# Experts' products in pairs, their rows turned by way of HBM, and the next attention's projections begun between them

## The chip, the cores and the metric

One NeuronCore of a Trainium2 chip runs the whole kernel. The metric is the device time in microseconds (us) of one execution, as the median of several. Engines: TensorE (PE) multiplies, with its weight loads shown apart as PEld; VectorE (DVE), ScalarE (ACT) and GpSimd (POOL) work on elements; SyncE (SP) issues all transfers (DMA) here, in order.

## The reference, cut to what matters

The input is `x` of 8 x 64 rows of 512 and a context of 8 x 1601 rows. Two layers of (attention over the context, attention or a time-mixing block over `x`, a feed-forward block) follow one another. The change lies where layer 0 ends and layer 1 begins:

```python
# layer 0, feed-forward: groups of 16 rows; 64 experts (16 x 4), each picks one row of each group
logits = einsum('...btd,des->...btes', grouped, controller) + tie
perm   = (logits == max(logits, axis=-3, keepdims=True))
sel    = einsum('...btd,...btes->...besd', grouped, perm)
inner  = relu(einsum('...besd,desf->...besf', sel, f1) + bias)     # 512 -> 64 for each expert
inter  = einsum('...besf,esfd->...besd', inner, f2)                # 64 -> 512 for each expert
x      = x + einsum('...besd,...btes->...btd', inter, perm)
# layer 1, attention over the context: 16 heads of 32
q = norm(x) @ Wq.T;  k = ctx @ Wk.T;  v = ctx @ Wv.T
x = x + softmax(scale * q k^T) v @ Wp.T + bp
```

There are 512 rows, so 32 groups and 64 x 32 pairs of an expert with its row.

## The kernel before, in words

Each engine has its own program, and they meet at semaphores. Tiles are 128 partitions by up to 512 columns, and `X`, the running rows, is four tiles of 128 rows. `R` is one large area of SBUF that every stage lays out anew by word offsets. PSUM is two halves of four banks, `SC` and `SB` (its banks are `BK`).

The middle stages take the banks of `SB` in a fixed ring of four. `JOBS` lists them in order with the engine that reads each ("d" DVE, "a" ACT); `open_bank` waits until the bank's last reader is through, `filled` and `readout` are the two semaphore levels of a job, and `evacuate` copies the jobs of one name out on the engine named. So `inter` 0, 2, ... are read by DVE and 1, 3, ... by ACT. `running(pe, us)` puts dummy 128 x 128 products on PE.

The order of PE's program around the change:

1. `sel` (L1071): the chosen rows, transposed, into 16 banks.
2. `inner` (L1084): four banks `q`, eight pairs of experts `j` in each. A pair is computed in two halves `r` of 64 weight columns, one in each half of the array, in four passes `k` over the 512 inputs. DVE adds the bias and applies the relu, into `inner`, cleared before so that the other expert's half of the columns is zero.
3. `inter` (L1097): f2 is the weight operand, in halves of 64 columns, the pair's `inner` is streamed (64 columns). The result has the 512 outputs on partitions, so it is not yet by rows; 16 banks, copied into `intert`.
4. `intert` (L1103): 64 transposes of 128 x 128 in 16 banks, copied into `intern`, where the partition is (group parity, expert).
5. `combination` (L1108): four products for each tile of rows, with `permx`, the choice, as weights of 32 columns. Then for each tile DVE adds to `X` and makes the norm's statistics, ACT the root, DVE the scaled row (`norm`), PE transposes it (`norm_transposes`, L415), ACT makes its high part (`norm_out`) and DVE its low part (`norm_low`). `normed` runs this tile by tile, with dummy products while PE waits.
6. `q4` (L1123): the queries in three passes. Products of the attention are f32 split in a high and a low part, so that each is three faster products (`three_passes`, L431).
7. `FIRST4`: the keys and values of batch 0. The context arrives transposed in four pieces (`load_chunk`), ACT makes the high part ("h" steps), DVE the low one (`split_low`), and then come jobs ("k", (piece, output blocks)) read by ACT into `keys` and ("v", tile) read by DVE into `vals`, 12 instructions each at the full width, in a ring of three banks. The same list of steps is walked by each engine, each doing its part; letters in `CONTROL4` take no bank.
8. Seven batches `BATCH4` of attention with the next batch's projections between, then `LAST4`, which also holds the last layers.

SP's queue goes: f1 in four transfers, f2 after `y2` 3, the raw weights of keys and values (`wraw`) once `inner` 3 is filled, the queries' weights and the bias row once `inter` 15 is filled, and the chunks once `intert` 15 is filled. POOL makes the low parts of these weights (L734) and both parts of the queries' weights (`split_weight`).

Of the kernel before, what the change touches and what calls it, by code (L numbers as in the profile page):

```python
# [25 lines left out]
EP = E // 2  # L26
G = B * T // NE
# [138 lines left out]
FIRST4 = [("h", 0), ("q", 0)] + EARLY4 + [("g", 0)]  # L166
BATCH4 = [attention(LATE4 + EARLY4, begins=b == 0, ahead=b < B - 2) for b in range(B - 1)]
CONTROL4 = "sohgq-mbpzelRNrEUA0C"
# [80 lines left out]
def mid_jobs():  # L249
# [32 lines left out]
    add("intert", 16, "da")  # L282
# [11 lines left out]
def build(nc, x, ctx_, ctx_end, W0, vecs, Wk, Wv, Wr, Wo, ctrl, f1, f2, Wq4, Wk4, Wv4,  # L294
# [7 lines left out]
    with ExitStack() as es:  # L302
# [40 lines left out]
        tiecol = sb("tiecol", [E, 1])  # L343
# [5 lines left out]
        minus_round = sb("minus_round", [P, 1])  # L349

        SC = psum("SC", [P, 2048])
        SB = psum("SB", [P, 2048])
        BK = [SB[:, k * 512:(k + 1) * 512] for k in range(4)]

# [97 lines left out]
        def spread_choice(eng, tt, name):  # L452

            inc(eng.tensor_tensor(permb[:, tt, :, :], permn[:, tt, :].unsqueeze(2).to_broadcast([P, E, 8]),
                                  gmask[:, :].unsqueeze(1).to_broadcast([P, E, 8]), ALU.mult), name)

# [13 lines left out]
        def by_batch(v):  # L470
# [15 lines left out]
        inner = Z[:, 1, :].rearrange("p (a k) -> p a k", k=2 * G)  # L486
        sel = R3.rearrange("p a c n -> p (a c n)").rearrange("p (c e g) -> p c e g", c=NC, g=G)
        intert = view(24576, 8192, NC, G, E)
        intern = view(16384, 8192, G // 2, D)

# [5 lines left out]
        batch4 = KW + VALS  # L496
        keys = [view(u * batch4, KW, HP, HK) for u in range(2)]
        vals = [view(u * batch4 + KW, VALS, KT_N, D) for u in range(2)]
        free4 = 2 * batch4

        low = [R[:, free4 + k * 2048:free4 + (k + 1) * 2048] for k in range(2)]
        wraw = R3[:, 0], R3[:, 2]

        low_r = [float32r(f"low{k}", free4 + k * 2048) for k in range(2)]
        high_r = [float32r("high0", free4 + 4096), float32r("high1", LT_AT)]
        wlow = [float32r(f"wlow{w}", R3_AT + 2 * w * 2048).rearrange("p (c n) -> p c n", n=D) for w in range(2)]
        whigh = [float32r(f"whigh{w}", R3_AT + (2 * w + 1) * 2048).rearrange("p (c n) -> p c n", n=D) for w in range(2)]
        wq4 = view(14336, 2048, NC, D)
        wp4 = view(0, 2048, NC, D)

        wq4_low, wq4_high, norm3_low = (cols(float32r(*a)) for a in (("wq4_low", 14336), ("wq4_high", 0),
                                                                    ("norm3_low", 2048)))
        norm_high = cols(high_r[1])
# [21 lines left out]
        short_keys = view(free4 + 6144, HP * MR, HP, MR)  # L535

        short_words = view(free4 + 6144, HP * MR + T)
        sums_inv = view(free4 + 6144 + HP * MR + T, NC * T)
# [13 lines left out]
        dt = [view(a, 2048, NC, D) for a in (2048, 4096, 6144, 8192)]  # L552
        normed4 = view(10752, 3 * D, 3, D)
        on5 = view(12288, 512, 2, 256)
        v5 = R[:, free4:free4 + 4096].rearrange("p (b j n) -> p b j n", j=HP // 2, n=P)
        k5 = view(free4 + 4096, 2048, NC, B * T)
# [10 lines left out]
        wq8 = view(10240, 512).bitcast(mybir.dt.int8).rearrange("p (c n) -> p c n", n=D)  # L567
        wq32 = view(10240, 512).bitcast(mybir.dt.int32).rearrange("p (c n) -> p c n", n=D // 4)
        wqt = view(12800, 1024).bitcast(BF16).rearrange("p (c n) -> p c n", n=D)
        xqt = view(13824, 1024).bitcast(BF16).rearrange("p (c n) -> p c n", n=D)  # L570
        xq = view(14848, 2048, NT, D)
        y6 = view(16896, 2048, NT, D)
        wsrow = view(18944, 512)
        bqrow = view(19456, 512)
# [10 lines left out]
        def _(sp):  # L585
# [42 lines left out]
            inc(sp.dma_start(tiecol[:, :], tie), "cw_in", 16)  # L628
# [8 lines left out]
            sp.wait_ge(*filled("inner", 3))  # L637
            inc(sp.dma_start(wraw[0], natural(Wk4)), "wk4_in", 16)
            inc(sp.dma_start(wraw[1], natural(Wv4)), "wv4_in", 16)
            sp.wait_ge(*filled("inter", 15))  # L640
            inc(sp.dma_start(wq4, natural(Wq4)), "wq4_in", 16)
            inc(sp.dma_start(bprow, bp4.unsqueeze(0).to_broadcast([P, D])), "bp_in", 16)

            def load_chunk(b, c):
                n, at = NC * piece_n(c, 1), NC * piece_keys(c).start
                inc(sp.dma_start(low[c % 2][:, 0:n], ctxt[b, :, at:at + n]), f"chunk_in{c % 2}", 16)

# [10 lines left out]
            def load_batch(b):  # L658
                for c in range(KC):
# [7 lines left out]
            sp.wait_ge(*filled("intert", 15))  # L667
# [21 lines left out]
        def _(pool):  # L689
# [18 lines left out]
            def split_weight(pool, w, high, low, name):  # L708

                inc(pool.tensor_copy(high, w), name)  # L710
                pool.wait_ge(sem(name), 1)
                inc(pool.tensor_tensor(low, w, high.bitcast(F32), ALU.subtract), name)
# [19 lines left out]
            for w in range(2):  # L732
                pool.wait_ge(sem("whigh"), w + 1)
                inc(pool.tensor_tensor(wlow[w], wraw[w], whigh[w].bitcast(F32), ALU.subtract), "wlow")  # L734
# [191 lines left out]
        def inter_dst(n):  # L926
            q, c = n // 4, n % 4
            return (intert[:, c, :, 16 * q:16 * q + 16],
                    bank("inter", n)[:, :].rearrange("p (e g) -> p g e", g=G))

# [14 lines left out]
        def steps4(eng, run):  # L945

            run(FIRST4, None, None)
            for b in range(B - 1):
# [4 lines left out]
        def _(pe):  # L953
# [135 lines left out]
            running(pe, 1.6)  # L1089
            pe.wait_ge(sem("f2_in"), 16)  # L1090
            for q in range(4):
                pe.wait_ge(*readout("inner", q))
                for c in range(NC):
                    bk = open_bank(pe, "inter", 4 * q + c)
                    for j in range(8):
                        for r in range(2):
                            last = pe.matmul(bk[64 * r:64 * r + 64, j * 64:(j + 1) * 64],  # L1097
                                             f2s[:, 8 * q + j, c * P + 64 * r:c * P + 64 * r + 64],
                                             inner[:, 8 * q + j, :], start=True, stop=True)
                    last.then_inc(filled("inter", 4 * q + c)[0], 1)  # L1100
            running(pe, 0.6)
            all_read(pe, "inter", 16)
            for gp in range(G // 2):  # L1103
                transposes(pe, "intert", gp, [(intert[:, c, 2 * gp:2 * gp + 2, :].rearrange("p g e -> p (g e)"), P, P)
                                              for c in range(NC)])
            pe.wait_ge(sem("permx"), 2)

            def combination(tt):  # L1108
                for i in range(4):
# [722 lines left out]
```

## Time and profile before

| | |
|---|---|
| median of 3 runs | 1179.06 us (1177.03 to 1179.46) |
| the profiled execution | 1176.5 us, its span 1174.7 us |
| PE busy | 1133.5 us, 96% |
| DVE, ACT, POOL busy | 619.1, 432.8, 333.6 us |
| granted PE clock, mean | 0.994 |
| instructions | 35,100, of them 16,122 products |
| read from HBM, written | 112.44 MB, 1.05 MB |

The time is that of the execution, the span is from the first to the last instruction of the trace. PE's products are pipelined and a product's shown end is modelled, so the spacing of starts tells more than the durations: a product's time includes its way through the array, some 165 ns over its streaming. An f32 product is two instructions, which together pass its columns four times; a product of split parts (fp32r) is one instruction and passes them once.

### The profile page before, as it was taken

To read this page: it belongs to the slowest core of one execution; us is meant where nothing else is said; L and a number is where in the kernel's file an instruction comes from. 1 tells how busy PE (TensorE), PEld (TensorE's weight loads), DVE (VectorE), ACT (ScalarE), POOL (GpSimd) and SP (SyncE) were. 2 spreads that over 40 slices of the span, in tenths; PEclk is the share of its full clock that TensorE was granted. 3 is DMA by queue.
4 is the path that set the end of the run, shared out by engine and by line. 5 is a ranking of instruction groups with operands and counts; after the bars stand their busy time and mean duration, and the time that the engine had idled before them with its cause. 6 is when DMAs were issued, how large, how long until landed. Compare 5 with 4: busy or idle time off the path is not lost.

```text
span 1174.7 us, 35100 instructions
## 1 busy us (share of the span) xinstructions
PE 1133.5 (96%) x16122; PEld 854.5 (73%) x16122; DVE 619.1 (53%) x977; ACT 432.8 (37%) x824; POOL 333.6 (28%) x364
## 2 busy tenths in 40 slices
PE   8988999999899999999999999999999999999896
PEld 5433454488688789788788888888888878856573
DVE  2011259555412655655655655655655565486667
ACT  1010153124333434443533534433533543435343
POOL 0000000025000242533344333424434342364512
PEclk9899999999999999999999999999999999999999
DMA  9999981254001101101100200200111110320000
GB/s 369 363 415 409 394 324 60 87 202 165 26 18 59 38 20 60 38 20 60 38 21 25 74 21 25 74 20 25 45 41 34 38 38 20 132 83 2 21 1 37
DMA packets 27620, 115.75 MB, mean 99 GB/s; under 512 B 2504, under 2 KB 3016, under 8 KB 22352
## 3 DMA queue, kind: packets, MB, share of 16 engines
q1 hardware_dynamic: 27472, 113.50, 26.1%
q8 instruction: 127, 2.08, 0.7%
q14 instruction: 21, 0.17, 0.0%
HBM read 112.44 MB, written 1.05 MB: 97 GB/s over the span
## 4 chain that ended last, share of the span: by engine, by line
PE 88%; DVE 5%; DMA 4%; issue 2%; ACT 1%; POOL 0%; SPq 0%; DVEq 0%; ACTq 0%; POOLq 0%
PE SB L431 50%; PE SB L422 7%; PE SC L1211 6%; PE SB L1240 4%; DMA R<-in_ctx_t 3%; PE SB L1276 2%; PE SC L996 2%; PE SC L1020 2%; PE SB L1084 1%; PE SB L1097 1%; PE SC L1203 1%; PE SB L1259 1%; PE SB L415 1%; PE SC L873 1%; PE SC L1220 1%
## 5 line engine op out<-in xcount | busy, mean ns | idle before, releaser
L1723 ACT COPY R<-SB 64x512 f32<-64x512 f32 (+1 forms) x224 | 116.3, 519 | 190.9 <-PE SB L431 189.0
L431 PE MATMUL SB<-high,whigh 128*128 128x512 f32 (+2 forms) x512 | 180.4, 352 | 1.0 <-ACT Z L444 1.0
L1526 DVE TENSOR_REDUCE LN<-SC 128x64 f32<-128x768 f32 x128 | 116.6, 952 | 119.8 <-PE SC L1211 119.7
L431 PE MATMUL SB<-high,wlow 128*128 128x512 f32 (+2 forms) x512 | 178.5, 349 | 0.0
L431 PE MATMUL SB<-low,whigh 128*128 128x512 f32 (+2 forms) x512 | 177.1, 346 | 0.0
L431 PE MATMUL SB<-wlow,high 128*128 128x512 f32 (+1 forms) x416 | 165.5, 398 | 0.0
L431 PE MATMUL SB<-whigh,high 128*128 128x512 f32 (+1 forms) x416 | 164.2, 395 | 0.0
L431 PE MATMUL SB<-whigh,low 128*128 128x512 f32 (+1 forms) x416 | 164.0, 394 | 0.0
L745 POOL TENSOR_TENSOR added<-LN 128x768 f32<-128x768 f32 x32 | 58.7, 1834 | 249.8 <-ACT LN L1755 249.8
L745 POOL TENSOR_TENSOR added<-Z 128x768 f32<-128x768 f32 x32 | 58.6, 1831 | 243.2 <-ACT Z L1755 243.2
L431 PEld LDWEIGHTS SB<-high,whigh 128*128 128x128 f32 x512 | 97.0, 189 | 13.6 <-issue 1.4
L431 PEld LDWEIGHTS SB<-high,wlow 128*128 128x128 f32 x512 | 97.0, 190 | 11.0
L431 PEld LDWEIGHTS SB<-low,whigh 128*128 128x128 f32 x512 | 96.8, 189 | 10.0
L1750 ACT COPY LN<-SC 128x128 f32<-128x128 f32 x64 | 17.0, 265 | 216.2 <-PE SC L1220 215.9
L1501 DVE COPY R<-SB 128x512 f32<-128x512 f32 (+1 forms) x104 | 71.1, 685 | 47.1 <-PE SB L431 46.1
L431 PEld LDWEIGHTS SB<-wlow,high 128*128 128x128 f32 (+1 forms) x416 | 76.8, 185 | 17.9
L431 PEld LDWEIGHTS SB<-whigh,low 128*128 128x128 f32 (+1 forms) x416 | 76.5, 184 | 18.0
L431 PEld LDWEIGHTS SB<-whigh,high 128*128 128x128 f32 (+1 forms) x416 | 76.8, 185 | 16.8
L1211 PE MATMUL SC<-qb,R 32*64 32x64 f32 x6144 | 87.1, 232 | 0.0
L1541 DVE TENSOR_TENSOR LN<-SC,LN 128x768 f32<-128x768 f32 x64 | 58.3, 952 | 50.1 <-ACT LN L1750 50.1
L1541 DVE TENSOR_TENSOR Z<-SC,LN 128x768 f32<-128x768 f32 x64 | 58.2, 950 | 42.8 <-ACT LN L1750 42.8
L1211 PEld LDWEIGHTS SC<-qb,R 32*64 32x64 f32 x6144 | 78.3, 130 | 0.0
(235 smaller groups left out, 1843.1 us busy)
## 6 DMA issues: line engine op xcount, KB each, us to landing
R<-in_ctx_t SPq DMA_DIRECT2D x32, 1024.0 KB, 6.0
R<-in_ctx SPq DMA_DIRECT2D x8, 3072.0 KB
R<-in_ctx_t SPq DMA_DIRECT2D x16, 644.0 KB, 7.0
R<-in_f SPq DMA_DIRECT2D x4, 2048.0 KB, 15.1
R<-in_f SPq DMA_DIRECT2D x1, 8192.0 KB, 25.0
R<-in_ctx_t SPq DMA_DIRECT2D x12, 512.0 KB, 3.6
R<-in_Wk SPq DMA_DIRECT2D x3, 1024.0 KB, 10.3
R<-in_Wv SPq DMA_DIRECT2D x3, 1024.0 KB, 8.8
```

The source lines that it names most:

```text
L422: last = pe.matmul(bk[:, :], lhs(k), rhs(k), start=k == 0, stop=k == NC - 1)
L431: last = pe.matmul(out_, lhs[a][:, k, :], rhs[b][:, k, :], start=n == 0, stop=n == 3 * NC - 1)
L745: inc(pool.tensor_tensor(added[:, :], p4_flat[w][0], p4_flat[w][1], ALU.add), "added4")
L996: last = pe.matmul(banks[w * T:(w + 1) * T, at + a:at + e], gt[:, k, p * P + w * T:p * P + (w + 1) * T], piece(slots[c][w], c)[:, k, a:e], ...
L1020: last = pe.matmul(banks[w * T:(w + 1) * T, out1_at], pt1[0:n, t, w * T:(w + 1) * T], cn[u][w][0:n, t, :], start=t == 0, stop=t == KT_N - 1)
L1211: last = pe.matmul(sc_half[g][64 * j:64 * j + 64, r, a * T:(a + 1) * T], keys[u][rows, x, a * P + 64 * j:a * P + 64 * j + 64], qb[rows, x, ...
L1240: last = pe.matmul(BK[3][j * HD:(j + 1) * HD, pairs * T:(pairs + 1) * T], vals[side][0:m, t, h * HD:(h + 1) * HD], probabilities, start=t ...
L1276: last = pe.matmul(bk[:, 0:at_.stop - at_.start], weight[:, k, ec * P:(ec + 1) * P], LT[:, k, at_], start=k == 0, stop=k == NC - 1)
L1501: inc(dve.tensor_copy(dst, src(BK[n])), f"read4_{n}")
L1526: inc(dve.tensor_reduce(tops[:, r * T:(r + 1) * T], sc_head[:, :, r, 0:6 * T].rearrange("p g (a q) -> p q g a", q=T), AX.XY, ALU.max), "ha ...
L1541: inc(dve.tensor_tensor(p4_half[x % 2][g], sc_half[g][:, :, 0:6 * T].rearrange("p r (a q) -> p r a q", q=T), top.unsqueeze(2).to_broadcast ...
L1723: last = act.copy(keys[nu][64 * half:64 * half + 64, pairs, first * P:first * P + full], src[:, :, 0:full])
```

## The change

- First products: one product of 128 weight columns for each pair and pass, in place of two of 64. `inner` now holds 32 columns for each pair (expert r of the pair on partitions 64r to 64r + 63), and isn't cleared.
- Second products: `inner` is the weight operand (64 rows, 32 columns), the rows of f2 are streamed, 512 columns. A group `m` has four pairs and two banks, one for each r; the result has (pair, group) on partitions and the 512 outputs in columns.
- The turn: each group is written to an array in HBM (`scratch`, 4 MB in eight transfers), and read back as `intern` in four, one for each tile of rows. Transposes, their copies and `intert` are gone.
- SP's queue: keys' weights and chunk 0 once `inner` 1 is filled; values' weights at `inner` 3; writes; reads, the queries' weights behind the second read; chunk 1 once `y3` 3 is filled.
- Chunk 0 is split before the list begins (ACT between its copies of `inter`, DVE after all of its own); the values' weights are cast on POOL instead of ACT, in pieces.
- `FIRST4` now starts with three keys' jobs, and the combinations ("c"), the norm's transposes ("t") and the queries ("q") stand between the jobs of piece 0, with banks of their own: the jobs of this list use `SC`. The dummy products of these stages are gone.
- The three passes run all inputs for one pair of parts before the next pair of parts. Areas of `R` are laid out anew; the tie is a row of 16 in place of a column.

The diff, cut (the new places of `R` and the list of waits for the tie left out):

```diff
+K0 = [x for x in BEGIN4 if x[0] == "k"]
+FIRST4 = [K0[0], K0[1], K0[2], ("c", 0), K0[3], ("c", 1), ("t", 0), ("v", 0), ("c", 2), ("t", 1), ("v", 1), ("c", 3),
+          ("t", 2), ("v", 2), ("t", 3), ("v", 3), ("h", 1), ("q", 0)] + REST4 + [("g", 0)]
...
-                k, (a, b) = n // 3, ((0, 0), (0, 1), (1, 0))[n % 3]
+                k, (a, b) = n % NC, ((0, 0), (1, 0), (0, 1))[n // NC]
...
+            sp.wait_ge(*filled("inner", 1))
+            inc(sp.dma_start(wraw[0], natural(Wk4)), "wk4_in", 16)
+            load_chunk(0, 0)
+            sp.wait_ge(*filled("inner", 3))
+            inc(sp.dma_start(wraw[1], natural(Wv4)), "wv4_in", 16)
+            turned = scratch.rearrange("a (r m j s) d -> m j (a r) (s d)", r=2, m=EM, j=4)
+            for m in range(EM):
+                for r in range(2):
+                    sp.wait_ge(*readout("inter", 2 * m + r))
+                inc(sp.dma_start(turned[m], inter[:, m].rearrange("p s d -> p (s d)")),
+                    "scratch_first" if m < 2 else "scratch_out", 16)
+            sp.wait_ge(sem("scratch_first"), 16 * 2)
+            sp.wait_ge(sem("scratch_out"), 16 * (EM - 2))
+            for tt in range(NT):
+                inc(sp.dma_start(intern[:, 4 * tt:4 * tt + 4, :], rows[:, 4 * tt:4 * tt + 4]), f"intern_in{tt}", 16)
+                if tt == 1:
+                    inc(sp.dma_start(wq4, natural(Wq4)), "wq4_in", 16)
...
-            sp.wait_ge(*filled("intert", 15))
+            sp.wait_ge(*filled("y3", NT - 1))
...
-                        for r in range(2):
-                            last = pe.matmul(bk[64 * r:64 * r + 64, j * 64:(j + 1) * 64],
-                                             f1s[q][:, k, j * P + 64 * r:j * P + 64 * r + 64],
-                                             sel[:, k, 2 * (8 * q + j):2 * (8 * q + j) + 2, :],
-                                             start=k == 0, stop=k == NC - 1)
+                        last = pe.matmul(bk[:, j * 2 * G:(j + 1) * 2 * G], f1s[q][:, k, j * P:(j + 1) * P],
+                                         sel[:, k, 2 * (8 * q + j):2 * (8 * q + j) + 2, :],
+                                         start=k == 0, stop=k == NC - 1)
...
-            running(pe, 1.6)
+            for m in range(EM):
+                if m % 2 == 0:
+                    pe.wait_ge(*readout("inner", m // 2))
+                bks = [open_bank(pe, "inter", 2 * m + r) for r in range(2)]
+                for j in range(4):
+                    for r in range(2):
+                        last = pe.matmul(bks[r][32 * j:32 * j + 32, :], inner[64 * r:64 * r + 64, 4 * m + j, :],
+                                         f2s[64 * r:64 * r + 64, 4 * m + j, :], start=True, stop=True)
...
+                        if steps is FIRST4 and c == 0 and (ecs[0] == 0 or kind == "v"):
+                            pe.wait_ge(sem("wlow"), 1 if kind == "k" else 2)
+                            pe.wait_ge(sem("split_first"), 1)
...
             evacuate(dve, "d", "inter", inter_dst)
+            dve.wait_ge(sem("high"), 1)
+            low_part(dve, cols(low_r[0]), cols(low[0]), cols(high_r[0]), "split_first")
...
+            act.wait_ge(*filled("inner", 3))
+            act.wait_ge(sem("wk4_in"), 16)
+            inc(act.copy(whigh[0], wraw[0]), "whigh")
+            evacuate(act, "a", "inter", inter_dst, range(0, 8))
+            act.wait_ge(sem("chunk_in0"), 16)
+            inc(act.copy(high_r[0], low[0]), "high")
+            evacuate(act, "a", "inter", inter_dst, range(8, 16))
...
+                        if steps is FIRST4 and (kind, x) == K0[2]:
+                            act.wait_ge(sem("scratch_first"), 16 * 2)
```

`low_part` subtracts the high part in four pieces of 512 columns.

## Rows read from the trace of the kernel before

**Rows 1.** The page's chain that ended last, shares by engine.
```profile
PE 88%; DVE 5%; DMA 4%; issue 2%; ACT 1%; POOL 0%; SPq 0%; DVEq 0%; ACTq 0%; POOLq 0%
```

**Rows 2.** The chain of waits, 205 to 410 us: start us, us, what.
```profile
247.81 4.54 PE SB L1084 x148
...
252.64 10.84 PE SB L1084 x362
...
269.44 11.30 PE SB L1097 x379
...
288.80 1.04 PE SB L1113 x8
...
292.15 0.61 DVE LN L813
...
304.61 11.18 PE SB L431 x48
...
316.80 63.75 PE SB L431 x319
```

**Rows 3.** PE's timeline: start us, busy us, line, shape, count [idle before <-releaser].
```profile
117.56 8.74 PE L996 MATMUL SB<-R,LT 128*64 128x512 f32 x33 [3.87 <-DMA R<-in_ctx_t]
...
293.40 1.06 PE L1113 MATMUL SB<-R,Z 128*32 128x512 f32 x8
...
294.40 1.38 PE L873 MATMUL SC<-ident 128*128 128x128 f32 x10
...
299.39 1.95 PE L873 MATMUL SC<-ident 128*128 128x128 f32 x16
...
346.83 0.39 PE L431 MATMUL SB<-high,whigh 128*128 128x512 f32 x1
...
349.55 0.39 PE L431 MATMUL SB<-whigh,high 128*128 128x512 f32 x1
...
352.27 0.39 PE L431 MATMUL SB<-whigh,high 128*128 128x512 f32 x1
...
391.11 1.25 PE L1211 MATMUL SC<-qb,R 32*64 32x64 f32 x92
```

**Rows 4.** Groups by line and form, 225 to 405 us: busy us, mean ns | idle.
```profile
L873 PEld LDWEIGHTS SC<-ident 128*128 128x128 f32 x132 | 15.7, 191 | 3.6 <-issue 3.3
...
L1084 PEld LDWEIGHTS SB<-R 128*64 128x64 f32 x512 | 15.1, 138 | 0.9 <-issue 0.9
...
L444 DVE COPY R<-SB 128x512 f32<-128x512 f32 x16 | 11.1, 691 | 13.2 <-PE SB L1097 10.2 <-PE SB L415 3.0
...
L444 ACT COPY R<-SB 128x512 f32<-128x512 f32 x16 | 9.4, 586 | 29.2 <-PE SB L1097 25.8 <-PE SB L415 3.4
...
L1507 DVE TENSOR_TENSOR low<-R,high 128x2048 fp32r<-128x2048 f32 x4 | 9.1, 2269 | 17.4 <-ACT high L1712 17.4
...
L1712 ACT CAST high<-R 128x2048 fp32r<-128x2048 f32 x4 | 7.6, 1908 | 0.0
...
L725 POOL TENSOR_TENSOR rows_low<-LN,rows_high 128x512 fp32r<-128x512 f32 x4 | 6.3, 1616 | 75.7 <-ACT rows_high L1692 75.7
```

**Rows 5.** Line 976, the `exb` products: ns min/median/max, first and last start.
```profile
L976 PE MATMUL SB<-vcols,Z x32: 167/250/333, 41.8 to 45.2; 128*128 128x1 f32 x32
```

**Rows 6.** Transfers, 150 to 420 us and the page: count, KB each, us to landing.
```profile
R<-in_ctx_t SPq DMA_DIRECT2D x4, 1024.0 KB, 4.9
...
out<-X SPq DMA_DIRECT2D x4, 256.0 KB, 2.0
```

**Rows 7.** Busy time by stretch: each engine, then granted PE clock, DMA share, GB/s.
```profile
50.00:51.00 1.00, 1.00 (x4) 0.27 (x2) 0.00 (x0) 0.00 (x0) 0.00 (x0) 0.50 1.07 308
...
115.00:118.00 3.00, 0.45 (x2) 0.33 (x4) 0.00 (x0) 0.00 (x0) 0.00 (x0) 0.82 1.00 415
...
118.00:121.00 3.00, 3.00 (x10) 0.94 (x8) 0.00 (x0) 0.00 (x0) 0.00 (x0) 0.61 1.01 411
...
232.00:240.00 8.00, 7.49 (x46) 5.38 (x45) 4.54 (x5) 2.55 (x5) 4.84 (x4) 1.00 1.04 393
```

More of the change, by code:

```diff
@@ L349, in build @@
         minus_round = sb("minus_round", [P, 1])
+        tierow = added[0:E, 0:NE]
         SC = psum("SC", [P, 2048])
@@ L455, in spread_choice, with low_part @@
                                   gmask[:, :].unsqueeze(1).to_broadcast([P, E, 8]), ALU.mult), name)
+        def low_part(eng, low_, raw, high, name):
+            for c in range(NC):
+                last = eng.tensor_tensor(low_[:, c, :], raw[:, c, :], high[:, c, :].bitcast(F32), ALU.subtract)
+            inc(last, name)
         def b4(bk):
@@ L658, in load_batch @@
             def load_batch(b):
-                for c in range(KC):
+                for c in range(b == 0, KC):
                     if c >= 2:
@@ L708, in split_weight @@
             def split_weight(pool, w, high, low, name):
-                inc(pool.tensor_copy(high, w), name)
+                for c in range(NC):
+                    last = pool.tensor_copy(high[:, c, :], w[:, c, :])
+                inc(last, name)
                 pool.wait_ge(sem(name), 1)
-                inc(pool.tensor_tensor(low, w, high.bitcast(F32), ALU.subtract), name)
+                for c in range(NC):
+                    last = pool.tensor_tensor(low[:, c, :], w[:, c, :], high[:, c, :].bitcast(F32), ALU.subtract)
+                inc(last, name)
             inc(pool.memset(causal[:, :], 0.0), "causal")
@@ L730, in _ @@
                 spread_choice(pool, tt, "permb_p")
-            for w in range(2):
-                pool.wait_ge(sem("whigh"), w + 1)
-                inc(pool.tensor_tensor(wlow[w], wraw[w], whigh[w].bitcast(F32), ALU.subtract), "wlow")
+            pool.wait_ge(sem("whigh"), 1)
+            low_part(pool, wlow[0], wraw[0], whigh[0], "wlow")
+            pool.wait_ge(sem("wv4_in"), 16)
+            for c in range(NC):
+                last = pool.tensor_copy(whigh[1][:, c, :], wraw[1][:, c, :])
+            inc(last, "whigh_v")
+            pool.wait_ge(sem("whigh_v"), 1)
+            low_part(pool, wlow[1], wraw[1], whigh[1], "wlow")
             pool.wait_ge(sem("wq4_in"), 16)
@@ L943, in probabilities_out1, with steps4 @@
                     inc(copy(pt1[0:MR, MF, :], bk[0:MR, 0:P]), f"read1_{g}")
-        def steps4(eng, run):
+        def steps4(eng, run, then=None):
             run(FIRST4, None, None)
+            if then:
+                then()
             for b in range(B - 1):
@@ L1088, in _ @@
                 last.then_inc(filled("inner", q)[0], 1)
-            running(pe, 1.6)
             pe.wait_ge(sem("f2_in"), 16)
[L1091 to L1105, printed above, removed]
+            for m in range(EM):
[6 more added lines that the diff above has]
+                                         f2s[64 * r:64 * r + 64, 4 * m + j, :], start=True, stop=True)
+                        if j == 3:
+                            last.then_inc(filled("inter", 2 * m + r)[0], 1)
@@ L1106, in _ @@
             pe.wait_ge(sem("permx"), 2)
             def combination(tt):
-                for i in range(4):
-                    pe.wait_ge(*readout("intert", 4 * tt + i))
+                pe.wait_ge(sem(f"intern_in{tt}"), 16)
                 bk = open_bank(pe, "y3", tt)
@@ L1510, in run4 @@
                 for kind, x in steps:
-                    if kind == "v":
+                    if kind == "c":
+                        norm(dve, 3, add_row("y3"), tiles=range(x, x + 1))
+                    elif kind == "t":
+                        norm_low(dve, 3, x, norm3_low)
+                    elif kind == "v":
                         n = tile_keys(x)
@@ L1518, in run4 @@
                         split_low(x)
+                        if steps is FIRST4 and x == KC - 1:
+                            dve.wait_ge(sem("bp_in"), 16)
+                            for tt in range(NT):
+                                inc(dve.tensor_tensor(X[:, tt, :], X[:, tt, :], bprow, ALU.add), "xbp")
                     elif kind == "l":
@@ L1694, in _ @@
             sel_out(act, "a", act.copy)
-            for w, name in enumerate(("wk4_in", "wv4_in")):
-                evacuate(act, "a", "inter", inter_dst, range(8 * w, 8 + 4 * w))
-                act.wait_ge(sem(name), 16)
-                inc(act.copy(whigh[w], wraw[w]), "whigh")
-            evacuate(act, "a", "inter", inter_dst, range(12, 16))
-            evacuate(act, "a", "intert", lambda gp: (intern[:, gp, :], bank("intert", gp)[:, :]))
-            norm_act(act, 3)
+            act.wait_ge(*filled("inner", 3))
[5 more added lines that the diff above has]
+            evacuate(act, "a", "inter", inter_dst, range(8, 16))
             def run4(steps, b, u):
@@ L1811, in laid_out @@
         "W0t": inputs["L0_xattn_W"].T, "ctx_t": ctx_t,
-        "tie": np.repeat(np.linspace(0.0, 1e-6, NE, dtype=np.float32), ES)[:, None],
+        "tie": np.tile(np.linspace(0.0, 1e-6, NE, dtype=np.float32), (E, 1)),
     }
```

168 lines of the change are left out of this document (81 added, 87 removed).

## Prediction

> **What bounds the kernel now.** I read the chain of waits first: TensorE (PE) carries 88% of it [rows 1], and no other engine carries more than 5%. So the question for every edit is what it does to PE between 247.8 us, where the experts' first products begin, and 380.5 us, where the first batch's projections end. Everything after that is the same list of steps. The chain inside that stretch [rows 2] then gives 132.7 us in eight pieces: first products 247.8 to 263.5 (15.7), filler 1.8, second products to 280.7 (15.5), filler and wait 0.9, 64 transposes 7.2 (what is left to 288.8), combination with the norm of four tiles 288.8 to 304.6 (15.8), the queries 11.2 and a wait of 1.0, projections 63.7. Only 48 + 319 instructions of the last two big pieces, some 75 us, are dense PE work; in the 15.8 us of combination and norm PE mostly waits for the norm on VectorE (DVE) and fills the time with dummy products. The reader should see there that one tile's add, statistics and scaling take 2.9 us (289.84 to 292.76), four times in a row.
>
> **First products.** Before, each pair of experts is computed in two halves of 64 weight columns, 512 instructions in 15.7 us, 30 ns each (an f32 product is two instructions). After, one product of 128 weight columns for each pair: 256 instructions, each 128 columns loaded and 64 columns streamed. The trace of before has no such shape, so I bracket it. From below: if streaming 64 columns sets the pace, it is that of two halves side by side less their overhead, at least 56 ns (I take half of the 112 ns of the 128-column filler [rows 3]: 256 x 0.056 = 14.3 us). From above: the filler streams 128 columns with 128 weight columns at (1.95 - 0.275) / 15 = 112 ns, which gives 28.6 us. Between them stands the load. The weight loads [rows 4] show 191 ns for 128 columns and 138 for 64: 53 ns for 64 columns, so about 106 ns of a load grows with its 128 columns. Two loads of 64 columns, 53 ns each, went in at one per 30 ns, so loads into the two halves of the array overlapped; a single load of 128 columns has nothing to overlap with. And one stage has the 128-column load with almost nothing to stream: the `exb` products, one moving column each, go at (45.2 - 41.8) / 31 = 110 ns [rows 5]. One moving column costs 110 and 128 cost 112, so 64 should cost 111: 256 x 0.111 = 28.4 us. I take that: **+12.7 us**.
>
> The Trainium skill (TensorE: Matmul & The Clock Gate, Part 3, The mechanism) goes further against this edit: a weight load overlaps products in flight only where the row group differs. By that, load and stream would add up, and the row of the filler disagrees, since its load (106) and its stream (107) together take 112; what it would give is the last rival.
>
> **Second products, turn and evacuation.** Let T be the end of the first products (247.8 + 28.4 = 276.2). 128 instructions stream 512 columns each through tiles of 64 rows by 32 columns, eight tiles to a group m of 16 instructions. Four column tiles side by side took 1.0 us for 8 such instructions [rows 3], so four run at once. That rows overlap too is shown by the scores: 92 instructions of 64 columns on eight tiles in 1.25 us, 11 ns each [rows 3], less than the 13 ns which four at once would give. I take 0.9 us for a group (bounds: 0.9, and 3.4 if only two tiles ran at once). What sets the pace is ScalarE (ACT): it casts the keys' weights first (as long as the cast of 1.91), evacuates inter 1, 3, 5, 7 (0.59 each), casts chunk 0 (1.91), then evacuates the other four [rows 4]. Group 2 needs inter 1 read, at T+2.6; groups 3 to 5 follow by T+6.2; group 6 needs inter 9, read after the cast, at T+7.7; group 7 ends at T+9.5. DVE evacuates inter 14 (0.69) to T+10.3 and only then makes the low part of chunk 0: 2.27 us in four pieces, say 2.4. The first keys' job starts at **T+12.8**. Behind that wait on PE is everything. The low part of the weights on POOL takes 6.4 in four pieces (as its 4 x 1.62 [rows 4]), from T+2 to T+8.4, in time; the values' weights are then cast and split to about T+18, used first at T+26.
>
> The old route from T was 1.8 + 15.5 + 0.9 + 7.2 + 15.8 + 11.2 + 1.0 + 63.7 = 117.1. The new one is 12.8, then the dense work: 63.7 of projections, 11.2 of queries, four combinations at 1.0 and four transposes of the norm at 0.55 (both from [rows 3], 293.40 to 294.40 and to the fillers): 6.2. Together 93.9. So **-23.2 us** if nothing stalls in between.
>
> **What must hide.** Eight writes of 512 KB go to HBM from about T+2.6 to T+10.3, beside 1 MB of the values' weights issued at T. At 393 GB/s [rows 7] 5.2 MB drain by T+14; with the landing, T+15. SP waits for all of them; queued behind that wait are the four reads of 1 MB, the queries' weights, the bias row and chunk 1. The first read lands 4.9 us later [rows 6], T+20 to T+21, the next at 2.7 us each: 23, then the queries' weights, then 28.5 and 31. PE asks for them after three keys' jobs of 2.73 us [rows 3] at T+21.0, and at T+24.7, 29.0 and 33.3. Cover equals need within a microsecond for the first, so no stall is booked, and the price is one for one if it is late. The norm fits as narrowly: per tile DVE has 2.9 of chain, 0.69 of low part and 0.69 of a value copy, 4.3 us, against PE's 1.0 + 0.55 + 2.73 = 4.3. The keys' third copy on ACT waits for two writes that are long down. The queries' weights are split on POOL (1.9 + 6.4) from about T+26 to T+35, needed at T+41. Chunk 1 is asked for at T+34.4, lands at T+39.3, is split by T+44, needed at T+52 after the queries. The 1.0 us wait after the queries goes, since their banks are not those of the projections.
>
> **The clock.** PE idles about 3.3 us before the first keys' job. The idle of 3.87 us before 117.56 [rows 3] was followed by a granted clock of 0.82 and 0.61 in two stretches of 3 us [rows 7], the lower of the two levels (1.2 of 2.4 GHz) for part of it. That cost about 0.2 + 3 x 0.39 = 1.4 us. I book **+1.4** (bounds 0 and, as after the `exb` stage whose clock stayed at 0.50 for some 6 us, 3.5).
>
> **At nothing.** The tie row is added by the same DVE pass; the cleared `inner` was behind PE's first products; the addresses in `R` move but no wait with them; the first load of batch 0 is earlier, with its bank of DMA idle. The three passes change order over 2,784 instructions, all after the queries' weights and context are whole: each ns would be 2.8 us. In the trace the keys' and the values' jobs repeat different operands and both take 2.72 us for 12 instructions [rows 3], so I put 0, with 1 ns either way as the bound.
>
> **Sum:** +12.7 - 23.2 + 1.4 = -9.1. The profiled execution took 1176.5 us around a span of 1174.7, the median is 1179.06; the difference carries over: **1170 us**.
>
> **Rivals.**
> 1. *The load does not bind*: two loads for each product could already run ahead in a way `exb` hides (its products add to one cell). Then 14.3 instead of 28.4: 14.1 us better, 1156. For it: 30 ns for half loads; against it: both bracketing rows. 0.15.
> 2. *The turn is late*: writes and reads in 2 and 4 KB pieces at less than 393. At 300 GB/s the writes end at T+19 and the first read at T+25, 4 us late: 1174. At 200, read 3 lands 20 us late: 1190. It decides at about 9 us late, near 255 GB/s. No row shows reads behind writes; the store of 256 KB in 2.0 us [rows 6] speaks against. 0.09.
> 3. *The clock falls in the first products* (the other side): PE streams only 53 of every 111 ns there, and after the `exb` stage, with one column a product, the clock was 0.50 [rows 7]. If it fell as late as there, after 3.6 us, the remaining 24.8 us would take twice as long: 1195. It decides from some 18 us at half clock. 0.08.
> 4. *Tiles of the second product run fewer at once*: four, 13.7 us, +4.2, 1174; two, 27.3, +17.8, 1188. 0.08.
> 5. *Load and stream add up*: 160 ns x 256 = 41.0, +12.6, 1183. 0.02, against it the filler's row. The rule of the Trainium skill named above (TensorE: Matmul & The Clock Gate) is this case.
>
> My own forecast has the rest, 0.58, with its range 1166 to 1176. A change of 0.2%, 2.4 us, is about what a measurement of this kernel tells from none. Faster: 0.58, 0.15, and about half of 2 and 4: 0.80; same 0.05; slower 0.15. The range 1155 to 1181 leaves out rivals 3 and 5, the far ends of 2 and 4 and a little of 1, together under 0.2.
>
> **What would show it.** First products of 128 weight columns at 111 ns each, 256 of them; PE's wait before the first keys' job about 3.3 us, released by DVE; ACT as the releaser of groups 2 and 6; intern read 0 landing near T+21; granted clock below 1 only after that wait. The forecast is wrong if the first products take 15 us, or the combinations wait for a DMA, or the clock is at 0.5 in the first products.

## The result, and the profile after

The changed kernel takes **1203.97 us** (median of 4 runs, 1203.12 to 1207.76) against 1179.26 us for the kernel before in the same comparison (4 runs, 1177.03 to 1181.24): a ratio of 1.0216, 95% interval 1.0188 to 1.0245. The forecast was 1170 with a range of 1155 to 1181 and 0.8 on faster. It was wrong by 34 us, in sign too.

The profiled execution took 1203.12 us, its span is 1201.1. From the page of the changed kernel: the clock in 40 slices, what was read and written, and the shares by engine of the chain that ended last.

```profile
PEclk9999999998699999999999999999999999999999
...
HBM read 116.64 MB, written 5.24 MB: 101 GB/s over the span
...
PE 86%; DMA 6%; DVE 4%; issue 2%; SPq 2%; ACT 0%; DVEq 0%; ACTq 0%
```

PE has fallen from the 88% of [rows 1] to 86 and DMA has risen from 4 to 6. The chain of waits, 205 to 440 us, says where:

```profile
246.91 28.78 PE SB L1121 x256
277.07 1.09 PE SB L1132 x16
...
282.94 2.53 SPq L667
285.59 4.68 SPq L667
290.37 4.69 SPq L667
295.15 4.73 SPq L667
299.98 23.54 DMA inter_rows<-R
323.58 5.73 DMA R<-inter_rows
329.35 1.93 PE SB L1142 x8
...
351.76 10.88 PE SB L439 x48
362.64 40.11 PE SC L439 x216
```

Between the second products (L1132) and the first combination (L1142) the chain leaves PE for 47 us (282.2 to 329.35). It goes through the writes that SP issues (L667), each issue 4.7 us after the one before, then through the last write, and through the read. The list `FIRST4` ends at 404.4, where it ended at 380.5 in [rows 2]: 23.8 of the span's 26.4 us. The timeline of the same kernel, with the idle time before each group and its releaser:

```profile
277.70 5.00 POOL L468 TENSOR_TENSOR wlow<-R,whigh 128x512 fp32r<-128x512 f32 x4 [35.00 <-ACT whigh L1730]
278.19 22.30 SPq L667 DMA_DIRECT2D inter_rows<-R  x8
...
285.01 6.27 POOL L468 TENSOR_TENSOR wlow<-R,whigh 128x512 fp32r<-128x512 f32 x4
...
285.97 5.86 DVE L468 TENSOR_TENSOR low<-R,high 128x512 fp32r<-128x512 f32 x4
...
291.93 2.04 PE L439 MATMUL SC<-high,whigh 128*128 128x512 f32 x4 [6.64 <-DVE low L468]
...
323.58 0.93 SPq L673 DMA_DIRECT2D R<-inter_rows  x2
...
329.35 1.93 PE L1142 MATMUL SB<-R,Z 128*32 128x512 f32 x8 [26.87 <-DMA R<-inter_rows]
```

And busy time by stretch (PE, PEld, DVE, ACT, POOL, then granted clock, DMA share, GB/s), to be held against [rows 7]:

```profile
285.00:290.00 5.00, 0.29 (x8) 0.00 (x0) 4.83 (x5) 0.72 (x2) 4.99 (x4) 0.96 0.26 104
290.00:295.00 5.00, 3.07 (x7) 2.48 (x8) 1.90 (x3) 0.00 (x0) 1.28 (x1) 0.50 0.27 108
...
315.00:320.00 5.00, 0.00 (x0) 0.00 (x0) 0.00 (x0) 0.00 (x0) 0.00 (x0) 0.50 0.26 106
...
330.00:335.00 5.00, 5.00 (x19) 3.05 (x12) 2.43 (x6) 0.20 (x1) 0.26 (x1) 0.60 1.05 398
```

The number to see is the share: while SP is writing, with nothing else on the queues, the DMA engines are busy 0.26 of their time and move 105 GB/s, whereas reads go at a share of 1.05 and 398 GB/s. A share that stays at a quarter suggests that four of the 16 engines work; the view gives only the mean over all 16. The write's destination, `turned[m]`, has j = 4 as its outermost dimension.

### The profile page after: what moved, and what is told of

Its sections match the earlier page's. It is cut to its first block, busy times and chain, and to the rows that moved or that the text cites. A ratio compares the mean times of both kernels' runs of the same rounds, so it can differ in the third digit from the quotient of the medians.

```text
span 1201.1 us, 33567 instructions
## 1 busy us (share of the span) xinstructions
PE 1128.3 (94%) x15345; PEld 841.4 (70%) x15346; DVE 615.7 (51%) x971; ACT 427.6 (36%) x815; POOL 339.5 (28%) x380
## 4 chain that ended last, share of the span: by engine, by line
PE 86%; DMA 6%; DVE 4%; issue 2%; SPq 2%; ACT 0%; DVEq 0%; ACTq 0%
PE SB L439 44%; PE SB L430 7%; PE SC L1245 6%; PE SC L439 5%; PE SB L1274 4%; DMA R<-in_ctx_t 3%; PE SB L1121 2%; PE SB L1310 2%; PE SC L1035 2%; DMA inter_rows<-R 2%; PE SC L1059 2%; SPq L667 1%; PE SC L1237 1%; PE SB L1293 1%; PE SC L1254 1%
## 5 line engine op out<-in xcount | busy, mean ns | idle before, releaser
L1756 ACT COPY R<-SB 64x512 f32<-64x512 f32 (+1 forms) x196 | 102.1, 521 | 149.1 <-PE SB L439 147.4
L439 PE MATMUL SB<-whigh,low 128*128 128x512 f32 (+1 forms) x376 | 106.2, 397 | 0.0
L439 PE MATMUL SB<-high,whigh 128*128 128x512 f32 (+2 forms) x448 | 106.0, 352 | 0.0
L439 PE MATMUL SB<-wlow,high 128*128 128x512 f32 (+1 forms) x376 | 105.9, 397 | 0.0
L439 PE MATMUL SB<-whigh,high 128*128 128x512 f32 (+1 forms) x376 | 105.9, 397 | 0.0
L439 PE MATMUL SB<-high,wlow 128*128 128x512 f32 (+2 forms) x448 | 104.6, 349 | 0.0
L439 PE MATMUL SB<-low,whigh 128*128 128x512 f32 (+2 forms) x448 | 103.9, 348 | 0.0
L439 PEld LDWEIGHTS SB<-high,whigh 128*128 128x128 f32 x448 | 75.7, 189 | 12.0
L439 PEld LDWEIGHTS SB<-high,wlow 128*128 128x128 f32 x448 | 75.7, 191 | 8.4
L439 PEld LDWEIGHTS SB<-low,whigh 128*128 128x128 f32 x448 | 74.4, 189 | 9.5
L439 PEld LDWEIGHTS SB<-wlow,high 128*128 128x128 f32 (+1 forms) x376 | 68.1, 184 | 16.4
```

Source lines behind the costliest of these rows:

```text
L1756: last = act.copy(keys[nu][64 * half:64 * half + 64, pairs, first * P:first * P + full], src[:, :, 0:full])
```

## The experiments

Theory A: a transfer is spread over as many DMA engines as its outermost dimension allows, here 4; the writes take 4 times as long as they could, and PE waits for them. The first rival: writes to HBM in 4 KB pieces are this slow anyway. T is the end of the first products in each kernel's own trace, and kernel 3 is that of experiment 3, and so on. The counts that waits compare with, changed to match the number of transfers, are left out of the diffs.

**1. Writes over all queues.** Each group's write is cut into four of 32 partitions.

```diff
-                inc(sp.dma_start(turned[m], inter[:, m].rearrange("p s d -> p (s d)")),
-                    "scratch_first" if m < 2 else "scratch_out", 16)
+                for j in range(4):
+                    inc(sp.dma_start(turned[m, j], inter[32 * j:32 * j + 32, m].rearrange("p s d -> p (s d)")),
+                        "scratch_first" if m < 2 else "scratch_out", 16)
```

> The changed kernel with each group's write cut in four, one for each 32 partitions, so that the outermost dimension of its destination is 32 and not 4. Theory A (the writes ran on 4 of 16 queues since their destination's outermost dimension was 4; that set their 105 GB/s and PE's wait of 26.9 us): DMA share in the writes well above 0.26, the last write down about T+16 (T is the end of the first products), PE's wait before the first combination 0 to 4 us, time 1204 - 24 = 1180 (1176 to 1184). Theory B (writes to HBM of this pattern are slow in themselves): share and rate as before, 1204. Theory C (32 issues at 0.4 to 0.6 us on SP replace the rate as the limit): the writes end by T+20, wait 5 to 8 us, 1184 to 1188.

Measured: 1176.01 us (10 runs, 1174.27 to 1178.06), ratio 0.9975 [0.9965, 0.9986]; 28 us less than the changed kernel. The stretches and the waits of this kernel:

```profile
285.00:290.00 5.00, 1.19 (x24) 0.18 (x8) 4.43 (x5) 1.17 (x2) 4.92 (x5) 0.99 0.93 273
290.00:295.00 5.00, 2.18 (x5) 1.82 (x6) 2.79 (x3) 0.00 (x0) 2.17 (x2) 0.50 0.94 278
...
L439 PE MATMUL SC<-high,whigh 128*128 128x512 f32 x32 | 9.7, 427 | 6.6 <-DVE low L468 6.6
...
L1143 PE MATMUL SB<-R,Z 128*32 128x512 f32 x32 | 4.3, 605 | 0.3 <-DMA R<-inter_rows 0.3
```

The share is 0.93, the wait for the read is 0.3 in place of 26.9. The same bytes in the same 4 KB pieces: the rival is out. But the rate is 273 to 278 GB/s, not the 393 of the forecast, so the last write lands at T+21, not at the T+15 of the forecast nor at the T+16 expected for this run.

**2, 3 and 4. The first products.** In halves of 64 again in the changed kernel (2), the same with the writes of 1 (3), and the reverse, the kernel before with only its products made 128 wide (4).

```diff
-                        last = pe.matmul(bk[:, j * 2 * G:(j + 1) * 2 * G], f1s[q][:, k, j * P:(j + 1) * P],
-                                         sel[:, k, 2 * (8 * q + j):2 * (8 * q + j) + 2, :],
+                        for r in range(2):
+                            last = pe.matmul(bk[64 * r:64 * r + 64, j * 64:(j + 1) * 64],
+                                             f1s[q][:, k, j * P + 64 * r:j * P + 64 * r + 64],
+                                             sel[:, k, 2 * (8 * q + j):2 * (8 * q + j) + 2, :],
```

> The changed kernel with the first products in halves of 64 weight columns again. Theory A (a load of 128 columns sets 112 ns an instruction; the writes then end 28 us after what was issued, whatever came before): first products 15.7 us instead of 28.8, everything behind moves up with them: 1204 - 13 = 1191. Rival: what is won is eaten by the wait for the turn, if that hangs on something that doesn't move: 1204.

> Both edits together. Theory A: the sum, 1180 - 13 = 1167 (1162 to 1171), so faster than the kernel before by about 1%. If the turn still makes PE wait (theory C of the first run): 1171 to 1175.

> The kernel before with the first products alone in pairs of 128 weight columns. Load-bound: 256 instructions at 112 ns, 28.8 instead of 15.7 us, all on PE's path: 1179 + 13 = 1192. If it was something else in the changed kernel that slowed these products (other addresses in R, the filler, the clock): 1179.

Measured: 2: 1190.55 us, ratio 1.0099 [1.0078, 1.0119], 13.4 less than the changed kernel. 3: **1163.75** us (1160.41 to 1166.27), ratio 0.9867 [0.9844, 0.9889]. 4: 1192.86 us, ratio 1.0112 [1.0095, 1.013], 13.7 us over the kernel before (1179.17). The wide products cost what the forecast said, in either kernel; the writes' 28.0 and the products' 13.4, each alone, make 41.4, and both together 40.2 (kernel 3). One line from the groups of 4, one from those of 3:

```profile
L1083 PE MATMUL SB<-R 128*128 128x64 f32 x256 | 28.8, 275 | 0.3 <-ACT R L922 0.3
```

```profile
L1123 PE MATMUL SB<-R 128*64 128x64 f32 x512 | 15.4, 222 | 0.3 <-ACT R L962 0.3
```

**5 to 8. What holds kernel 3.** PE waits 6.5 us for DVE's low part there, whose four pieces take 5.7 us where 2.4 were booked, and then works for some 5 us at a lower clock (0.54 from 275 to 280 us, 0.78 from 280 to 285). Three suspects, on kernel 3: (5) POOL, which splits the values' weights at the same time, is held back until DVE is done; (6) PE gets 6.2 us of dummy products in the wait, for the clock; (7) writes of two groups each, 16 transfers of 256 KB, to free SP sooner; (8) all three, with 3.0 us of dummies.

```diff
             pool.wait_ge(sem("wv4_in"), 16)
+            pool.wait_ge(sem("split_first"), 1)
...
+            running(pe, 6.2)
             for n in range(SKIP4):
                 inc(pe.nop(), f"full4_{n}")
...
+            turned = scratch.rearrange("a (r m j s) d -> j (a r) m (s d)", r=2, m=EM, j=4)
+            for m in range(0, EM, 2):
...
+                    inc(sp.dma_start(turned[j, :, m:m + 2], inter[32 * j:32 * j + 32, m:m + 2].rearrange("p m s d -> p m (s d)")),
```

> e3_both, with POOL waiting for the low part of chunk 0 before it casts and splits the values' weights. Theory P (two engines at work on SBUF slow one another: DVE's four pieces took 1.46 us each while POOL subtracted, not the 0.57 of its other split): the four pieces take 2.3 to 2.5 us, the first keys' job starts 3.4 us sooner after T, POOL's own pieces get shorter too. Rival Q (the pieces of 512 columns are slow in themselves): still 5.8 us. On the time, theory Q2 (the turn through HBM is nearly as late as the keys' jobs: in e1_turn16 PE still waited 0.3 us for it): the 3.4 us come back as a wait before the first combination, time equal within 1.5 us, 1162 to 1164. If the turn has slack: 1160.

> e3_both, with 6.2 us of dummy products while PE waits for the low part. If the idle is what lowered the clock to 0.5: granted clock 1.00 through the first keys' jobs, which take 8.2 us and not 10.7. Theory Q2: PE then waits some 2.3 us for the turn, time within 1 us of e3_both. Otherwise 2.5 us faster.

> e3_both, with two groups in each write, 16 transfers of 256 KB in place of 32 of 128 KB. Theory C (after the spread over 16 queues, SP's 0.42 us an issue limits the turn: its last issue came 9 us after the last copy): the last write is down at T+16.5 instead of T+21, and nothing gains from it while the keys' jobs start at T+16 and run at half clock: time as e3_both, 1163, within 1 us. Rival (the DMA's own rate of 280 GB/s is the limit): the last write still at T+20.

> All three edits on e3_both (3.0 us of dummy products, since the wait is that long without the contention). Keys' jobs at T+12.9, clock at 1.00, first combination at T+21 to T+22.5 instead of T+27: 4.5 to 6 us faster than e3_both, 1157 to 1159. If the three limits are not the only ones there: above 1161.

Measured: 1166.02, 1164.43, **1162.56** and 1165.48 us, ratios 0.9889 [0.986, 0.9917], 0.9868 [0.9838, 0.9898], 0.9859 [0.9834, 0.9884] and 0.9884 [0.9857, 0.9911]. None is apart from kernel 3's 0.9867. Two of the three suspects were real and their removal worked locally: POOL (5) and the clock (6). SP's issuing (7) was not. Timeline of 5:

```profile
275.44 2.49 DVE L468 TENSOR_TENSOR low<-R,high 128x512 fp32r<-128x512 f32 x4
278.03 1.61 PE L439 MATMUL SC<-high,whigh 128*128 128x512 f32 x4 [3.27 <-DVE low L468]
...
291.98 1.79 PE L1146 MATMUL SB<-R,Z 128*32 128x512 f32 x8 [3.89 <-DMA R<-inter_rows]
```

DVE's low part takes 2.49 us once POOL is quiet, the booked 2.4, and the wait for DVE halves; but 3.9 us appear as a wait for the read. In 6 the keys' jobs start at 282.88 at a clock of 1.00 and take 8.2 us, as expected, and PE then waits 2.7 us for the read. In 8, with all three:

```profile
277.17 1.17 PE L439 MATMUL SC<-high,whigh 128*128 128x512 f32 x4 [0.17 <-issue]
...
286.51 0.93 SPq L674 DMA_DIRECT2D R<-inter_rows  x2
...
292.31 1.93 PE L1146 MATMUL SB<-R,Z 128*32 128x512 f32 x8 [6.72 <-DMA R<-inter_rows]
```

PE starts at T+13.1, at full clock, and the whole gain returns as 6.7 us of waiting, behind which the clock is at 0.50 (290 to 296 us): the fall has moved, not gone. The first combination stands at T+26.8 in kernel 1, T+27.0 in 3, 27.1 in 5, 27.5 in 6, 28.2 in 7 and 8. The turn takes 27 to 28 us whatever the engines do: last write at T+21.1 to T+22.5, read 5.7 to 5.9. I had expected 1157 to 1159 of 8 and 1162 to 1164 of 5, and missed both. Experiment 7 says that SP's issuing (32 issues in 16.8 us, 16 in 15.0) isn't the limit: with half the issues the reads started at T+22.5 and not at the T+16.5 expected, later even than the T+21.1 of kernel 3. Its time came out as expected, but not for the reason given. What is left is the rival named there, the rate of the transfers themselves: in kernel 7 the DMA engines are busy 0.95 to 0.97 of the time between 270 and 280 us, and 4.2 MB at the 256 to 271 GB/s of that stretch are 15.5 to 16.4 us (an estimate), behind the 1 MB of the values' weights.

**9. The dose.** Writes cut in two, with an outermost dimension of 2.

```diff
+                for h in range(2):
+                    inc(sp.dma_start(turned[m, 2 * h:2 * h + 2], inter[64 * h:64 * h + 64, m].rearrange("p s d -> p (s d)")),
```

> The changed kernel, with each group's write cut into two transfers whose outermost dimension is 2 (it was one transfer with 4 there). Theory A, the outermost dimension sets how many of the 16 queues a transfer uses: a transfer keeps 2 queues busy, 1/8 of them, so the DMA share falls from the 0.26 of the changed kernel to about 0.13 while one transfer is served after the other and the rate from 105 to about 53 GB/s; if both halves of a group land on different queues at once, share and rate stay at 0.26 and 105. By the first, the last write lands at about T+85 and the time is about 1243 us; by the second, 1204. Rival, the size of a transfer (256 KB in place of 512) sets its rate: a rate unlike both, and above all a higher one than 105, as the four transfers of 128 KB of the first experiment had 280.

Measured: 1243.85 us, one run. Its stretches and its timeline:

```profile
300.00:320.00 20.00, 3.30 (x15) 2.41 (x13) 0.00 (x0) 2.33 (x4) 0.00 (x0) 0.68 0.13 53
320.00:340.00 20.00, 0.00 (x0) 0.00 (x0) 0.00 (x0) 0.00 (x0) 0.00 (x0) 0.50 0.13 53
```

```profile
279.39 60.49 SPq L668 DMA_DIRECT2D inter_rows<-R  x16
...
368.76 1.94 PE L1143 MATMUL SB<-R,Z 128*32 128x512 f32 x8 [65.46 <-DMA R<-inter_rows]
```

A share of 0.13 and 53 GB/s, with transfers half as big as the changed kernel's. Outermost dimension 2, 4 and 32 give 53, 105 and about 277 GB/s, shares of 0.13, 0.26 and 0.93, and a first combination at T+91.9, T+53.8 and T+26.8. Two transfers on the queue did not spread over two sets of engines. Theory A holds at three doses, and a rate set by the size of a transfer (256, 512, 128 KB) is out, since it would have to rise and fall. Kernels 7 and 9 are the cleanest pair: 16 writes of 256 KB each, with 32 and 2 outermost. In 9 the share is 0.13 and the rate 53 GB/s, in 7 they are 0.95 and 271:

```profile
270.00:275.00 5.00, 1.95 (x32) 0.58 (x32) 3.24 (x5) 1.96 (x4) 4.92 (x6) 0.98 0.95 271
```

**10. Load or stream.** As 3, each half streaming only its own expert's 32 columns.

```diff
-                            last = pe.matmul(bk[64 * r:64 * r + 64, j * 64:(j + 1) * 64],
-                                             sel[:, k, 2 * (8 * q + j):2 * (8 * q + j) + 2, :],
+                            last = pe.matmul(bk[64 * r:64 * r + 64, j * 64 + 32 * r:j * 64 + 32 * r + 32],
+                                             sel[:, k, 2 * (8 * q + j) + r, :],
```

> As the third experiment (writes of 32 partitions each and first products in halves of 64 weight columns), but each half of the array streams the 32 columns of its own expert alone, half of the 64. If the load of 64 columns, two of them in flight in the two halves, sets the pace of 30 ns, nothing moves: first products 512 x 0.030 = 15.4 us and the time that of the third experiment, 1164 (within 3 us). If streaming sets it (64 columns, 53 ns in each half, two halves side by side, 27 each), they go at some 16 to 20 ns, 9 to 10 us, and the time is 5 to 6 us less, 1158.

Measured: 1165.26 us, ratio 0.9881 [0.9855, 0.9907], the time of kernel 3. Its chain of waits, and that of kernel 3:

```profile
246.45 4.51 PE SB L1123 x148
251.19 7.60 PE SB L1123 x254
259.75 5.29 PE SB L1123 x109
```

```profile
245.65 4.54 PE SB L1123 x148
250.20 10.85 PE SB L1123 x363
```

148 instructions take 4.51 us with 32 columns and 4.54 with 64, 30 ns each: streaming does not set the pace, and the load is what is left. (The last 109 are slower in 10 because the clock fell: it is at 0.50 from 262 to 266 us, behind a pause of 0.96 us in which PE waited for nothing that the profile shows. Kernel 12, whose products are those of 3, took 4.95 for them, with 0.50 from 261.5 to 264.5 us behind a pause of 2.25.)

**11. The order of the three passes**, alone, in the kernel before.

```diff
-                k, (a, b) = n // 3, ((0, 0), (0, 1), (1, 0))[n % 3]
+                k, (a, b) = n % NC, ((0, 0), (1, 0), (0, 1))[n // NC]
```

> The kernel before, with the order of the three passes alone as the change has it (all inputs for one pair of parts, then the next). The prediction booked 0 and a bound of 1 ns each over 2,784 instructions, 2.8 us. Theory: nothing, 1179 within 1.5 us, the batches' period 92.20 us. Rival: the order costs the 0.13 us for each batch by which the changed kernel's period of 92.33 exceeds the 92.20 of before; then the period is 92.33 here too and the time some 1 us more.

Measured: 1177.98 us against 1177.8, ratio 1.0001 [0.9988, 1.0014], and a period of 92.20 us from the products at 405.85 to those at 498.05. The 0 of the forecast is right as far as the kernel before can show it. The 0.13 us a batch (92.33, in the changed kernel and in 3) come from another part, not tracked down.

**12. The list in another order**, on 8 without its dummies.

```diff
-FIRST4 = [K0[0], K0[1], K0[2], ("c", 0), K0[3], ("c", 1), ("t", 0), ("v", 0), ("c", 2), ("t", 1), ("v", 1), ("c", 3),
-          ("t", 2), ("v", 2), ("t", 3), ("v", 3), ("h", 1), ("q", 0)] + REST4 + [("g", 0)]
+FIRST4 = [K0[0], K0[1], K0[2], K0[3], ("v", 0), ("c", 0), ("c", 1), ("t", 0), ("v", 1), ("c", 2), ("t", 1), ("c", 3),
+          ("v", 2), ("t", 2), ("v", 3), ("t", 3), ("h", 1), ("q", 0)] + REST4 + [("g", 0)]
```

> As the eighth experiment (small writes, halves, writes of two groups, the values' low parts after the context's), without the filler, and with the list in another order: all four keys' jobs and the first values' job stand ahead of the first combination. Theory, the turn through HBM is the limit (first rows read at T+28, where TensorE waited 6.7 us for them in the eighth): the two jobs of 2.73 us fill that wait, at most 5 us less, about 1160 to 1162, and the wait for the first rows shrinks to 1 to 2 us. Rival, what the jobs cover there they leave bare behind: three values' jobs are left for a norm of 4 x 4.3 us, waits of 1 to 2 us before each transpose of the norm take the place, and the time is that of the eighth, 1165, or above.

Measured: 1163.8 us (1161.75 to 1166.06), ratio 0.9877 [0.9858, 0.9895], no better than 3 and above the 1160 to 1162 expected. From its timeline:

```profile
295.73 1.92 PE L1146 MATMUL SB<-R,Z 128*32 128x512 f32 x16
...
300.17 0.65 PE L423 MATMUL SB<-ident,LN 128*128 128x128 f32 x4 [2.51 <-DVE LN L854]
...
314.47 1.16 PE L439 MATMUL SB<-norm_high,wq_high 128*128 128x512 f32 x4 [1.71 <-DVE norm_low L895]
```

The wait for the read is gone, and in its place stand 2.5 us before the first transpose and 1.7 before the queries, both released by DVE: the jobs that cover the turn no longer cover the norm. The queries begin at T+48.4 here, T+47.3 in 3.

## Why the prediction was wrong, step by step

**The step that failed is the write rate in "What must hide".** It booked eight writes at 393 GB/s, drained by T+14 and landed by T+15, and so no stall. They went at 105 GB/s, the last landed at T+48, and PE waited 26.9 us. The 393 was the rate of reads of whole matrices into 128 partitions; the row did not speak of a transfer with another outermost dimension. Rival 2 had the consequence, a late turn that PE waits for, but another cause, the small pieces, which experiment 1 rules out as the cause of the 105. Its turning point, near 255 GB/s, agrees with kernel 1, which at about 277 is just faster than before. But its worst case was 200 GB/s, and it held the store of 256 KB in 2.0 us [rows 6] against itself, a store of whole rows from 128 partitions and so no evidence for a pattern with 4 outermost. The error was to price the transfer by its bytes and its piece size and not by its shape. The Trainium skill has the rule (DMA: Bandwidth & Descriptors, Why a DMA increments its semaphore by 16 and not by 1): the number of engines is the largest up to 16 that divides the outermost non-1 dimension of both access patterns. The traces agree: 0.13, 0.26 and 0.93 of the engines for 2, 4 and 32.

**The keys' job was 3.5 us later than booked** (291.93 with T at 275.6, T+16.3 for T+12.8). The evacuations kept their times, the term of 2.4 for the low part did not: 5.86 us beside POOL's subtraction of the same kind, 2.49 without it (experiment 5). Both were in the forecast's own schedule at the same moment and priced apart. The Trainium skill says why it can be (SBUF — State Buffer, SBUF: two separate sides): POOL and DVE share a pair of ports, which an instruction holds alone if it is POOL's, or DVE's with two inputs in SBUF. The trace agrees in part: 0.57 us a piece [rows 4] became 1.46, and POOL's pieces went from 1.25 to 1.57. But if each piece held the ports for all of its time, one of each would take 0.62 + 1.25 = 1.87 us (an estimate from the times alone in kernel 5); one of each took about 1.5. So the slowing is shown, and the lock as its cause is not.

**The clock** was booked at +1.4 for one fall. There were two (stretches at 0.50 behind DVE's wait and behind the long one). From 291.93 to 404.35 the dense work took 112.4 us, 85.5 without the wait of 26.9, against the 81.1 summed from full-speed rows: 4.4 for the two.

**Right.** First products at 111 ns each: 28.78 us for 28.4, and the +12.7 came out at 13.4 and 13.7 in experiments 2 and 4. Rival 1 is out: the load did bind (for the halves, 10 shows that streaming does not), the clock stayed at 1.00 in them (rival 3 out), and load and stream did not add up (rival 5 out, and with it what the rule on row groups in the Trainium skill, TensorE: Matmul & The Clock Gate, Part 3, The mechanism, would give here: 160 ns an instruction by the forecast's sum, where the trace has 112). Second products ended with their copies' pace at T+9.7 for 9.5, 32 instructions in 1.95 us, so a group of 16 in about 1.0 for 0.9, and ACT released groups 2 and 6 as said; rival 4 is out. The norm hid where the list put it, the pass order cost nothing. The forecast's first paragraph speaks of eight pieces and lists nine, which add up to 132.8 and not 132.7; nothing hangs on it.

**The sum.** Against the forecast's end of `FIRST4` (T+93.9, +1.4 for the clock), the measured T+128.8 is 33.4 more: 3.5 + 26.9 + 3.0. T itself was 0.6 early. Behind it, the batches add 0.7 us and the last stages 1.9; together that is 35.4 of the 35.5 us by which the span (1201.1) missed 1165.6. In the last stages one stretch of 8 us (1121 to 1129) has a granted clock of 0.80, which is at 1.00 in kernel 3 and at 0.79 in kernel 5; why is open.

**What the idea is worth.** With writes over all engines and the old first products, 1162.6 to 1163.8 us, 1.3 to 1.4% faster than before (kernels 3 and 7). So the new route is worth 15.4 us in kernel 3, and 16.6 in kernel 1 (3.2 less than before, in spite of 13.4 for the wide products), of the 21.8 that the forecast gave it with its clock term. One dimension of a transfer and a wider operand hid it.

## What to carry to other kernels

Price a transfer by its shape first: read the outermost dimension of both sides, and look for a row of a transfer with the same one before taking a rate; a DMA share that stays at a small fraction while transfers are queued (0.13 and 0.26 here) is what this fault looked like. When a stall is filled from one side, ask what the next limit is: here two real costs, the slowed subtraction and the clock, were removed singly and together for no gain, because the turn through HBM took 27 us of its own. Two engines' work that a schedule puts at the same time has to be priced together.

## What the runs showed of the hardware that was not expected

- Writes from SBUF to HBM with all engines busy (share 0.93 to 0.96) went at 273 to 279 GB/s in kernels 1 and 3, where reads of the same data went at 369 to 398. Four engines made 105, 26 each, so 16 are 1.5 times short of four times that. Why is open.
- A subtraction on DVE with both inputs in SBUF went from 0.57 or 0.62 us to 1.46 beside POOL's. POOL's own went from 1.25 to 1.57.
- T differed between kernels with the same first products: 261.1, 264.9, 266.5, 262.0, 264.1 and 266.1 us in 3, 5, 6, 7, 8 and 12. A part is there already when the first products begin (245.7 in kernel 3 to 248.2 in 6). In 5, 6, 8, 10 and 12 there is also a pause of 1.0 to 2.25 us in which PE waited for nothing the profile shows, each time with the last 109 of the 512 instructions to go and begun while the keys' weights and chunk 0 were in transfer, as in this row of 12's chain:

```profile
258.97 2.25 issue
```

The spans, 1158.6 to 1163.3 us, follow T: span less T is 896 to 899 in all six. So kernels 3 to 8 can't be ranked against each other. What causes the pause is open; that the place is the same in five kernels speaks for one cause. The clock fell behind it in 10 and 12 (0.50) and stayed at 1.00 in 6.
